# Row maxima sixteen row pairs ahead instead of eighteen, and one operand load to a chunk instead of two, in a fused attention and feed-forward kernel

## The reference

```
x = hidden_states                                    # (16, 512, 128)
n = layernorm(x)
q, k, v = heads(n @ Wq.T + bq), heads(n @ Wk.T + bk), heads(n @ Wv.T + bv)
idx = clip(pos_k - pos_q, -20, 20) + 20
attn = softmax((q @ k.T + einsum('bhqd,qkd->bhqk', q, rel_k[idx])) / sqrt(8))
w = attn @ v + einsum('bhqk,qkd->bhqd', attn, rel_v[idx])
x = x + merge(w) @ Wo.T + bo
n = layernorm(x)
x = x + (silu(n @ wg.T) * (n @ wu.T)) @ wd.T         # hidden 384, int weights / 127
```

## Time and profile before

| what | value |
|---|---|
| median of 3 runs | 1260.71 us (1256.79 to 1262.96) |
| the profiled execution, whole time | 1265.17 us |
| its span, from first to last instruction | 1263.4 us |
| TensorE busy | 1207.8 us, 96% of the span |
| VectorE busy | 912.2 us, 72% |
| ScalarE busy | 735.7 us, 58% |
| GpSimd busy | 578.1 us, 46% |
| DMA queue q1, share of 16 engines | 22.0% |

### The profile page before, as it was taken

One profiled execution on the slowest core, in us unless ns is written; L12 is line 12 of the kernel. 1 busy time (PEld: TensorE's weight loads), 2 busy tenths in 40 slices (PEclk: granted clock), 3 DMA queues, 4 the chain that ended last, 5 costly groups with the idle time before them and its releaser, 6 DMA issues. The chain is left out here.

```text
span 1263.4 us, 60291 instructions
## 1 busy us (share of the span) xinstructions
PE 1207.8 (96%) x27042; PEld 828.2 (66%) x27042; DVE 912.2 (72%) x1747; ACT 735.7 (58%) x1382; POOL 578.1 (46%) x1083
## 2 busy tenths in 40 slices
PE   6988999999999999999999999999999999999998
PEld 4554466767666666666666666676666677666675
DVE  6886877777777767777777777777777776156664
ACT  6885255656666656566666666666666566523322
POOL 5986554444445444443435454444454444022221
PEclk9998999999999989999999999999999999999999
DMA  5776202120203030303021221213030300023221
GB/s 169 228 233 201 54 5 45 34 55 24 63 20 68 12 69 10 70 9 69 22 57 36 52 50 37 57 30 72 20 69 11 70 10 10 12 68 98 77 76 51
DMA packets 101001, 76.52 MB, mean 61 GB/s; under 512 B 12744, under 2 KB 96520, under 8 KB 100744
## 3 DMA queue, kind: packets, MB, share of 16 engines
q1 hardware_dynamic: 100744, 72.67, 22.0%
HBM read 44.86 MB, written 26.21 MB: 56 GB/s over the span
## 5 line engine op out<-in xcount | busy, mean ns | idle before, releaser
L1210 DVE TENSOR_REDUCE b_mx<-b_a 128x1 f32<-128x512 f32 x1024 | 658.5, 685 | 220.5 <-PE b_a L877 218.7
L1155 ACT ACTIVATE b_p<-b_s 128x512 f32<-128x512 f32 x1024 | 569.6, 595 | 366.6 <-PE b_s L936 224.6
L823 POOL TENSOR_TENSOR qd<-q,one 48x512 bf16<-48x512 bf16 x256 | 266.2, 1040 | 453.2 <-PE b_s L936 433.9
L992 PE MATMUL b_pv<-b_p,vg 128*32 128x256 f32 x4096 | 276.3, 383 | 0.0
L936 PE MATMUL b_s<-qd,z 112*128 112x32 bf16 (+1 forms) x6016 | 248.7, 188 | 3.4 <-issue 3.3
L936 PEld LDWEIGHTS b_s<-qd,z 112*128 112x128 bf16 (+1 forms) x6016 | 204.1, 98 | 13.6 <-issue 3.8
L877 PE MATMUL b_a<-k,q 48*128 48x512 bf16 x1024 | 199.8, 386 | 11.3 <-DVE b_mx L1210 3.0
L898 PE MATMUL b_s<-q,k 54*128 54x64 bf16 (+5 forms) x4096 | 186.2, 205 | 8.2 <-DMA q<-b_mt 7.1
L898 PEld LDWEIGHTS b_s<-q,k 54*128 54x128 bf16 (+1 forms) x4096 | 111.4, 95 | 103.0 <-PE b_s L898 29.8
L992 PEld LDWEIGHTS b_pv<-b_p,vg 128*32 128x32 f32 x4096 | 117.4, 109 | 59.8 <-issue 20.3
L945 PE MATMUL b_s<-q,k 118*128 118x64 bf16 x2048 | 104.7, 195 | 2.6 <-issue 2.6
(11 more groups left out here) (146 smaller groups left out, 1263.3 us busy)
## 6 DMA issues: line engine op xcount, KB each, us to landing
x<-in_x SPq DMA_DIRECT2D x24, 256.0 KB, 3.4
scratch_qop<-a_parts SPq DMA_DIRECT2D x16, 384.0 KB, 2.6
scratch_kop<-a_parts SPq DMA_DIRECT2D x16, 384.0 KB, 3.4
k<-scratch_kop SPq DMA_DIRECT2D x32, 192.0 KB
q<-scratch_qop SPq DMA_DIRECT2D x32, 192.0 KB
scratch_v<-a_vr SPq DMA_DIRECT2D x16, 256.0 KB, 3.5
k<-scratch_kop SPq DMA_DIRECT2D x32, 128.0 KB
q<-scratch_qop SPq DMA_DIRECT2D x32, 128.0 KB
```

Of the source, the lines that this page charges most:

```text
L823: nc.gpsimd.tensor_tensor(dst, src, one, ALU.mult).then_inc(s["qd_ready"], 1)
L992: nc.tensor.matmul(PV[V32 * a:V32 * (a + 1), g * PT:(g + 1) * PT], v[:, side, half, t, 2 * a + g, :], PR[pos][:, 4 * a + 2 * half + g, :], ...
L1155: nc.scalar.activation(out, src, ACT.Exp, scale=SCALE).then_inc(s["p_ready"], 1)
L1210: nc.vector.tensor_reduce(MX[unit.v % 2][:, h:h + 1], PA[(HP * n + hp) % NBANK][:, :], AX_X, ALU.max, negate=True).then_inc(s["a_used"], 1)
```

## The change

The lead of the row pairs becomes 16: the last two entries of `EXTRA` (chunks 4 and 12 of pair 1) go. The table `PIECES` goes as well, and the 12 loads are issued one to a chunk in chunks 0 to 11, with the values at chunk 12 instead of chunk 8. All line numbers behind L40 fall by one.

```diff
-PIECES = ((0, 1), (2,), (3,), (4, 5), (6, 7), (8, 9), (10, 11))
...
-EXTRA = (0, 1, 12, 14, CHUNKS + 4, CHUNKS + 12)
+EXTRA = (0, 1, 12, 14)
...
                 for c in range(CHUNKS):
-                    if ahead and c < len(PIECES):
+                    if ahead and c < NLOAD:
                         sp.wait_ge(s["s_ready"], PB2 * pair + 2 * c + 1)
-                        load_score_operands(sp, k, d, batch + 1, (batch + 1) % 2, PIECES[c])
-                    if ahead and c == len(PIECES) + 1:
+                        load_score_operands(sp, k, d, batch + 1, (batch + 1) % 2, [c])
+                    if ahead and c == NLOAD:
                         sp.wait_ge(s["s_ready"], PB2 * pair + 2 * c + 1)
                         load_values(sp, k, d, batch + 1, (batch + 1) % 2)
```

## The result

The changed kernel takes **1255.34 us** (median of 20 runs, 1248.5 to 1263.2), the kernel before 1263.14 us in the same comparison (20 runs, 1256.79 to 1275.0). The ratio is **0.9927** (95% interval 0.9904 to 0.9951): faster by 0.7%, or by 7.8 us (0.6%) between the two medians. The sign and the wide range of the prediction (1243 to 1265) hold. The forecast of 1247 and its own band (1243 to 1252) do not: the gain is about half of the 13 to 16 us forecast (13 against the median of 1260.7 known then, 16 against 1263.1), and 1255.3 is where rival (C) stood, 1256.

A forecast was written before the change was run, and what follows sets the result against it. TensorE was taken as the bound, with 20.0 us to gain in the loading pairs. From the profiled 1265.2 us, 1265.2 - 20.0 + 3.5 - 1.2 = 1247.5, called 1247; own band 1243 to 1252, range 1243 to 1265.

The forecast's parts named there:

- rival (C): Instruction fetches stay late: guard-row waits at chunk 6 go, other stops and half-clock stretches stay; 1256 or 1252 us; chance 0.18.
- What bounds the kernel: TensorE, busy 1207.8 of 1263.4 us; at most 20.0 us to gain, in the 14 loading pairs, 1.4 each.
- The guard rows of chunk 2: TensorE's waits at chunk 6 go, with no query load queued ahead of these rows: -8 us, between -6 and -10.
- The short stops and half-clock stretches in the middle of the pair: Stops and half-clock stretches, 12 us in all, shrink to 3.5 as loads spread: -8.5 us, between 0 and -12.
- What is late next: At chunk 0, guard rows of chunk 13 land 26.8 us after the pair's first load, needed at 27.9: 0.
- The slow loads: Query loads on three or two engines, 3.3 or 2.9 us each, two pairs of 6.2, done at t = 23.4.
- The values and the guard rows behind them: End of a loading pair's queue: values take 1.9 us, guard rows 1.5 more, landing at t = 26.8.
- The lead of 16 and its slack: GpSimd's last guard part ends 2.6 us ahead of TensorE's transpose, so the shorter lead costs 0.
- The two row pairs of pair 1: Two extra row pairs leave pair 1, -2.0 us, and come back in pair 30, +0.8: net -1.2.
- The sum: Whole kernel, from the profiled 1265.2 us: 1247.5, called 1247; all dips leave, so the base doesn't matter.
- The signs that the prediction named: For: guard-row weight-load waits drop from 15 to 1 or 2; against: one-engine share at t 28, issue stops, chunks 6-8.
- rival (B): The queue keeps its length: TensorE stands 2.1 us at chunk 0 in every loading pair; 1273 us, slower; chance 0.27.

The follow-up runs named there:

- the bunched run: Kernel before with the lead of 16 and the first query load moved behind the guard rows, loads not spread one to a chunk: ratio 1.0010.
- the run with the loads only: Changed kernel with the old lead of 18, loads still one to a chunk: 1294.1 us, ratio 1.0234.

## Why the prediction was right, and where it was off

**What bounds the kernel**: right. Quiet pairs take 29.1 us in all kernels with a lead of 16 or 18, and without the loads the 14 loading pairs have 0.4 us above them left. No run gained more than that one, 19.2 us by the medians, where the prediction had 20.0 in the loading pairs.

**The guard rows of chunk 2** (-8): right. The loading pairs lost 7.1 us at chunk 6 and now nothing; 9.9 us of waits of the weight loads became 0.4, and the bunched run shows that the order of issue alone does this.

**The short stops and half-clock stretches in the middle of the pair** (-8.5): right for the profiled execution. Chunks 7 to 11 lost 12.0 us before and lose 3.0 after, and I had kept 3.5. The bunched run, with 11.2, shows that it is the spreading that does this. The prediction had only argued that these stops are late blocks of instructions, and the views give the blocks' queue q8 only in total, but the traces' single records bear it out. Queue q8 moved 214 blocks for some 54,800 weight loads and matrix products, so a block holds 256 of them. In the 13 profiles other than that of the lead of 14, TensorE's matrix products have 73 stops of 0.15 us or more between 160 and 1040 us that are put down to "issue" and are not at a row pair. All 73 come a whole number of blocks apart in TensorE's row (give or take 3, for records that are missing), and each ends 1.2 to 2.1 us behind the end of a block's transfer. The stop of 2.00 us in pair 4 of the kernel before ends at 281.06 and has the transfer 278.24 to 279.78 ahead of it, which began 6.9 us behind the one before, where 4.6 is the median. So TensorE had no stock of blocks that would cover such a delay, and the doubt on this in rival (C) falls. The 14 stops for the operands in the run with the loads only are called "issue" too, and none of them is at a block's border. Which load holds a block back stays open.

**What is late next** is the step whose size was wrong. I named the right place and both ends, and took the sum: guard rows at 26.8, in time by 1.1. They came at 27.9 on average and at up to 29.4, and are needed at 27.9: TensorE waited in six of 14 pairs, 4.3 us in this profile, and in seven, 4.7 us, in the second. Two terms of the sum were off, in opposite directions:

- *The slow loads.* The sum has them done at t = 23.4 (it counts two of the last three query loads and leaves out that of 64 KB), which is 16.9 us behind the first query load. The operands were complete at 26.3, 19.8 behind it, close to the 21.0 of the kernel before. That "one load to a chunk hardly lets a queue form" was the reading that failed; for these loads what was carried over from pair 12 was nearer.
- *The values and the guard rows behind them.* The sum adds 1.9 + 1.5 = 3.4 us. Measured are 27.9 - 26.3 = 1.6: the values landed 1.2 us behind the operands, and the guard rows 0.4 behind the values. This took back 1.8 of the 2.9 us by luck.

A mean just on time, with single pairs 1.1 us earlier to 1.5 us later, is late in nearly half of the cases. A term for "in time by 1.1" needs the spread of the 14 pairs, which the trace had (guard rows from t = 25.6 to 29.2 in the kernel before), and not one pair.

**The lead of 16 and its slack** (0, 2.6 to spare): right; in the changed kernel's pair 13 the last guard part ends 2.65 us ahead of the transpose, and a lead of 14 costs 0.96 us a pair.

**The two row pairs of pair 1** (-1.2): the lead alone gave 2 us by the medians, with an interval that holds 0; not contradicted.

**The sum.** Against its own profile the forecast was 1247.5 and the measurement 1248.5. Most of the miss against the median is in the next step, "as all dips leave the sum, the base doesn't matter". The dips left that one execution: its mean granted clock is 0.997, that of the median of the 20 runs 0.993. The kernel before has 0.991, in its profile and in the median of the later runs. A clock mean lower by 0.004 is 5 us, most of the 6.8 between the profile and the median. So the change took away some 2.5 us of loss by the clock in a typical run, not the 6.8 of the two dips, and the remaining 5 us of the gain are, by subtraction, stops. Where the dips of a typical run lie isn't known: the two executions profiled were the fastest of their 20 and of their 7. **One profile is one draw** for anything that comes and goes by execution. That 1255.3 is the number of rival (C) is chance in the main: (C) had the middle of the pair unchanged, and there 12.0 us became 3.0.

**The signs that the prediction named.** For it: the waits for the guard rows of chunk 2 are down to one, and no half-clock stretch is left in the loading pairs of this execution. Against it, both signs of being wrong were seen: the share of one engine at t = 27.4 to 28.4 behind pair 8, and four stops with "issue" at about chunks 6 to 8, though of 0.21 to 0.52 us only. The waits at chunk 0, the sign of rival (B), came six times and not 14. The stores of chunk 11 were no sign at all: in the changed kernel SyncE holds them back behind the load of that chunk, so that most distances alternate between about 30.1 and 28.1 us.

## What to carry to other kernels

A queue of transfers that is waited for at two places can trade one stall for the other: moving the slow load behind the first small copy cost as much at the second until the loads were also spread out. Before shifting a lead or a load, write down for each waiting point when it is needed and when the queue gets there in every period, and look at the late half of them. The cheapest step found here was the one the change had left: what nobody waits for (the values) goes behind what somebody does, 0.9909 to 0.9862.

## What the runs showed of the hardware

- In stretches with loads that read the same rows several times, 45 to 77 GB/s were moved, at shares of 0.14 and 0.23 of the 16 engines and at 0.41 to 0.74. What holds them there is open.
- TensorE's stops without a named cause are at the borders of its instruction blocks of 16 KB: 73 of 73 outside the row pairs, each ending 1.2 to 2.1 us behind the end of a block's transfer.
- With a stop of about 1 us in each pair of 30.7 us, eight stretches of 3.4 us at half clock came, four of them 92.2 us behind the one before, which is every third pair (209.12 and 301.28 are the first two). Each costs 1.7 us. A single stop of 2.05 us in the kernel before was followed by none, and one of 2.00 by 6.8 us.
- A wait for the operands' semaphore is listed as "issue", a wait for the guard rows by its transfer, on the same line.
